# Moving the state matmuls of a fused attention and feed-forward kernel from around the transposes to between the gate/up pairs

## The chip, the core and the metric

The kernel runs on one core of a Trainium2 chip. A core has five engines that run their own instruction streams and meet at semaphores: TensorE (PE, matrix products into PSUM), VectorE (DVE), ScalarE (ACT), GpSimd (POOL) and SyncE (SP, which issues transfers). The metric is the device time of one execution in microseconds (us), the median of three runs: 507.38 us before the change (507.33 to 507.74).

## What is computed

The input `x` is 8 sequences of 1024 tokens with 256 channels, fp32. With `xn = layernorm(x)` the output is

```python
x + attn(xn) + ffn(xn)

# attn: linear attention with 16 heads of 16 channels
q = elu(xn @ Wq.T) + 1;  k = elu(xn @ Wk.T) + 1;  v = xn @ Wv.T
kv_state = einsum('bhnd,bhne->bhde', k, v);  k_state = k.sum(tokens)
attn_out = einsum('bhnd,bhde->bhne', q, kv_state) / max(einsum('bhnd,bhd->bhn', q, k_state), 1e-6)
local    = three-tap convolution of xn along the tokens, per channel
attn     = (attn_out + local) @ Wp.T + bp

# ffn: int weights times 1/127, hidden size 768
ffn = (silu(xn @ wg.T) * (xn @ wu.T)) @ wd.T
```

`kv_state` and `k_state` sum over all 1024 tokens of a sequence, so the attention output of a sequence can only be formed when all its keys and values have been seen.

## The kernel before

A sequence `b` is worked off in two halves `c = 0, 1` of 512 tokens, 16 halves in all, one after the other. Halves of sequences 2 to 6 stand in a hardware loop (`Fori`), the others are written out. fp32 precision comes from fp16 pairs: a tensor is held as a high and a low part (`xh`, `xl`), and a product is made as three fp16 products (two where a weight is exact in fp16).

In each half PE issues, in this order (function names as in the code):

- `project_kv(0)`, `query` for the same half of the sequence before (with `state`, as fp32), `project_kv(1)`, `project_q()`
- `accumulate(0)`: the state matmuls of the first two token tiles, `v_sb` with `k_sb` as 32-column weights in four column groups of the array, 16 instructions (32 in the trace) into PSUM bank 6
- `transpose_attn` twice: 8 transposes of `attn` into banks 5 and 7
- `accumulate(1)`: the state matmuls of the other two tiles
- `gate_up(0)` to `gate_up(5)`: each a gate/up pair of 8 matmuls of 512 columns into two PSUM banks. Even pairs use banks 2 and 3, odd ones 0 and 1. Between them stand `project_y` (after `gate_up(4)`, and after `gate_up(5)`)
- `down(0)`, `down(1)`: 48 matmuls of 256 columns

What the other engines do around these pairs sets when a pair may start. `gate_up(0)` waits for `v_ready`, `gate_up(1)` for `q_read` (DVE has read the banks of `project_q`), and every later `gate_up(j)` for `hid_ready` of pair `j-2`, because it overwrites the banks which that pair filled. After `project_q`, ACT runs `q_neg` (L526), `q_exp` (L529), loads the table for silu (L557), and then `silu(0)` (L536), which needs `gu_done` of pair 0. DVE runs `q_relu` (L858), `put_y` twice (L806), then `hidden(0)` (L896, makes `hid` from `act_g` and the up bank), `put_q` (L865), `hidden(1)` and so on.

`accumulate` waits for `k_ready`, `v_ready`, `acc_kept` and `attn_ready`. Its result is read by `put_state` on DVE (L873, L878), which stands behind `hidden_low(5)`; in the very last half, where nothing follows, it stands earlier, before `hidden(2)`. In that last half ("not ahead") `project_y` stands after `gate_up(2)` and after `gate_up(3)`, and the queries of the last sequence come after `gate_up(4)`.

Of the kernel before, what the change touches and what calls it, by code (L numbers as in the profile page):

```python
# [39 lines left out]
def build(nc, x, wqT, wkT, wvT, wpT, bp, conv_w, conv_b, wgT, wuT, wdT, out):  # L40
# [16 lines left out]
    def at(b, c, per_step, k):  # L57

        return b * (CB * per_step) + (c * per_step + k)

    with ExitStack() as ctx:
# [92 lines left out]
        def gate_bank(j):  # L154
            return 2 * ((j + 1) % 2)
# [873 lines left out]
        def _(pe):  # L1029
            def tiles_of(bank):  # L1030
                return ps[:, bank, :].rearrange("p (i t) -> p i t", i=TILES)
# [3 lines left out]
            def three(dst, stat, mov):  # L1035

                for n, (s, m) in enumerate(TERMS):
                    for k in range(KT):
                        ins = nc.tensor.matmul(dst, stat(s, k), mov(m, k), start=(n == 0 and k == 0),  # L1039
                                               stop=(n == len(TERMS) - 1 and k == KT - 1))  # L1040
                return ins
# [63 lines left out]
            def transpose_attn(b, c, p, banks):  # L1105

                pe.wait_ge(attn_ready, at(b, c, 2, p + 1))
                for i in range(2):
                    for k in range(KT):
                        ins = nc.tensor.transpose(ps[:, banks[p], k * PAIR + i * P:k * PAIR + (i + 1) * P],  # L1110
                                                  attn[:, 2 * p + i, k * P:(k + 1) * P], ident[:, :])
                ins.then_inc(yT_done, 1)

            def project_y(b, c, p, banks):
                pe.wait_ge(yl_ready, at(b, c, 2, p + 1))
                for i in range(2):
                    t = slice((2 * p + i) * P, (2 * p + i + 1) * P)
                    ins = three(ps[:, banks[p], i * D:(i + 1) * D], lambda s, k: (yh, yl)[s][:, k, t],
                                lambda m, k: p_w[m][:, k, :])
                ins.then_inc(wp_done, 1)  # L1120

            def step(b, c, attend, ahead):
# [27 lines left out]
                def accumulate(p):  # L1150

                    pe.wait_ge(k_ready, at(b, c, 2, p + 1))
                    pe.wait_ge(v_ready, at(b, c, 2, p + 1))
                    if p == 0 and past:

                        pe.wait_ge(acc_kept, at(b, c, 1, 0))
                    if p == 0 and attend:

                        pe.wait_ge(attn_ready, at(b - 1, c, 2, 2))
                    for i in (2 * p, 2 * p + 1):  # L1160
                        for k in range(KT):
                            for g in range(G):
                                rows = slice(g * GROUP, (g + 1) * GROUP)
                                ins = nc.tensor.matmul(ps[rows, STATE, k * VW:(k + 1) * VW],  # L1164
                                                       k_sb[:, i, k * P + g * GROUP:k * P + (g + 1) * GROUP],
                                                       v_sb[:, i, k * G + g, :], start=(i == 0 and k == 0),
                                                       stop=(i == TILES - 1), skip_group_check=True,
                                                       tile_position=(0, g * GROUP))
                    ins.then_inc(acc_done, 1)

                def project_q():

                    if past:
                        pe.wait_ge(v_ready, at(b, c, 2, 1))
                    else:
                        pe.wait_ge(first_xl, 1)
                        pe.wait_ge(q_hi, 1)
                        pe.wait_ge(q_lo, 1)
                    bank = 0 if past else FIRST_Q
                    for m in range(KT):  # L1180
                        ins = three(tiles_of(bank + m), lambda s, k: q_w[s][:, k, m * P:(m + 1) * P],
                                    lambda s, k: x2[s][:, c, :, k, :])
                    ins.then_inc(q_done, 1)

                def gate_up(j):

                    if j == 0:

                        pe.wait_ge(v_ready, at(b, c, 2, 2))
                    elif j == 1 and not past:  # L1190

                        pe.wait_ge(v_ready, 1)
                    elif j == 1:

                        pe.wait_ge(q_read, at(b, c, 1, 1))
                    else:
                        pe.wait_ge(hid_ready, at(b, c, J, j - 1))
                    for n, w in enumerate((g_w, u_w)):
                        dst = tiles_of(gate_bank(j) + n)
                        cols = slice(j * P, (j + 1) * P)  # L1200
                        for k in range(KT):
                            nc.tensor.matmul(dst, w[0][:, k, cols], xh[:, c, :, k, :], start=(k == 0), stop=False)  # L1202
                    with pe.If(is_wide["gate_up"]):
                        pe.wait_ge(gate_up_lo, 2)
                        for n, w in enumerate((g_w, u_w)):
                            for k in range(KT):
                                nc.tensor.matmul(tiles_of(gate_bank(j) + n), w[1][:, k, j * P:(j + 1) * P],
                                                 xh[:, c, :, k, :], start=False, stop=False)
                    for n, w in enumerate((g_w, u_w)):
                        for k in range(KT):  # L1210
                            ins = nc.tensor.matmul(tiles_of(gate_bank(j) + n), w[0][:, k, j * P:(j + 1) * P],  # L1211
                                                   xl[:, c, :, k, :], start=False, stop=(k == KT - 1))
                    ins.then_inc(gu_done, 1)
# [72 lines left out]
                    query(b - 1, c, 1, QKV)  # L1286
                project_kv(1)
                project_q()
                accumulate(0)
                if attend:  # L1290
                    transpose_attn(b - 1, c, 0, TURNED)
                    transpose_attn(b - 1, c, 1, TURNED)
                accumulate(1)
                gate_up(0)
                gate_up(1)
                if isinstance(b, int) and b == 1 and c == 0:

                    pe.wait_ge(p_hi, 1)
                    pe.wait_ge(p_lo, 1)
                if ahead:  # L1300
                    for j in range(2, J):
                        gate_up(j)
                        if attend and j == Y_PROJECT:

                            project_y(b - 1, c, 0, WP)
                    if attend:

                        project_y(b - 1, c, 1, WP)

                    pe.wait_ge(hid_ready, at(b, c, J, J - 1))  # L1310
                    down(0, DOWN)
                    if past and not attend:

                        pe.wait_ge(res_ready, at(b, c - 1, 2, 2))

                    down(1, DOWN)
                else:
                    first, second = 0, 1
                    gate_up(2)
                    project_y(b - 1, c, 0, WP)  # L1320
                    gate_up(3)
                    project_y(b - 1, c, 1, WP)
                    gate_up(4)

                    pe.wait_ge(out_ready, at(b - 1, c, 2, 2))
                    query(b, first, 0, LAST_QKV[0])
                    query(b, first, 1, LAST_QKV[0])
                    gate_up(5)

                    pe.wait_ge(hid_ready, at(b, c, J, J - 1))  # L1330
                    query(b, second, 0, LAST_QKV[1])
                    transpose_attn(b, first, 0, LAST_YT[0])

                    pe.wait_ge(hid_ready, at(b, c, J, J))
                    query(b, second, 1, LAST_QKV[1])
                    transpose_attn(b, first, 1, LAST_YT[0])
                    down(0, LAST_DOWN)

                    project_y(b, first, 0, LAST_WP[0])
                    project_y(b, first, 1, LAST_WP[0])  # L1340

                    transpose_attn(b, second, 0, LAST_YT[1])
                    transpose_attn(b, second, 1, LAST_YT[1])
                    down(1, LAST_DOWN)

                    project_y(b, second, 0, LAST_WP[1])
                    project_y(b, second, 1, LAST_WP[1])

            is_wide = {}
            run(pe, step)  # L1350


# [23 lines left out]
```

## Time and profile before

| | before |
|---|---|
| median of 3 runs | 507.38 us (507.33 to 507.74) |
| the profiled execution: its own time | 506.9 us |
| its span, first to last instruction | 505.3 us |
| mean granted TensorE clock | 0.999 of full speed |
| PE busy | 491.4 us, 97% |
| DVE busy | 430.5 us, 85% |
| ACT busy | 334.3 us, 66% |
| state matmuls (L1164) on the chain that ended last | 2.3% |

The profile is of one execution. "Busy" is the time in which an engine had an instruction in flight. A PE row of the timeline groups instructions that ran back to back; its duration includes the way of the last result through the array, so the step from one row's start to the next row's start is what a group costs PE in a stream, and the duration is longer than that. In brackets stands how long the engine was idle before a row and what ended the wait. PEld is the weight load of PE. Times in the timeline count from the start of the span.

### The profile page before, as it was taken

The numbers are of one execution on the slowest core, as the hardware profiler recorded it, in microseconds if no ns is written. First come the engines' busy times: TensorE is split into PE (matmuls) and PEld (weight loads), VectorE is DVE, ScalarE is ACT, GpSimd is POOL, SyncE is SP. The second block draws the span as 40 slices with busy tenths as digits, with TensorE's granted clock in tenths as the row PEclk, the third lists the DMA queues.
The fourth block names the chain that finished last, engine by engine and source line by source line (L and its number), as shares of the span: only waits on it lengthen the run. The fifth ranks groups of instructions, "written<-read, shape, count | busy, mean of one in ns | idle before, by whom it ended". The sixth has DMA issues, their size and how long they took to land.

```text
span 505.3 us, 11017 instructions
## 1 busy us (share of the span) xinstructions
PE 491.4 (97%) x3968; PEld 306.1 (61%) x3968; DVE 430.5 (85%) x833; ACT 334.3 (66%) x522; POOL 144.7 (29%) x152
## 2 busy tenths in 40 slices
PE   7888999999999999999999999999999999999997
PEld 6545364755747566474756657475565756657576
DVE  4889898889888898988889888889888889897786
ACT  2676866667485775757667485667758576674770
POOL 3563415140321405033140502314041141401050
PEclk9999999999999999999999999999999999999999
DMA  8573434333524423252352325233342442233012
GB/s 307 183 91 77 86 82 87 68 111 51 151 43 111 99 45 125 41 166 42 83 125 42 125 42 164 43 82 100 54 138 42 126 82 42 87 50 74 3 42 84
DMA packets 68653, 45.36 MB, mean 90 GB/s; under 512 B 33424, under 2 KB 68112, under 8 KB 68624
## 3 DMA queue, kind: packets, MB, share of 16 engines
q1 hardware_dynamic: 59360, 35.79, 25.2%
q0 software_dynamic: 8448, 8.39, 11.0%
q10 hardware_dynamic: 816, 0.79, 0.5%
q8 instruction: 19, 0.31, 0.3%
q14 instruction: 10, 0.08, 0.0%
HBM read 20.32 MB, written 8.39 MB: 57 GB/s over the span
## 4 chain that ended last, share of the span: by engine, by line
PE 88%; DVE 5%; ACT 3%; DMA 2%; issue 1%; ACTq 0%; DVEq 0%
PE ps L1202 16%; PE ps L1039 16%; PE ps L1211 15%; PE ps L1221 15%; PE ps L1145 15%; PE ps L1101 5%; PE ps L1110 3%; PE ps L1164 2%; DMA wv_raw<-in_L_attn_Wv_dram 2%; DVE maxima L665 1%; DVE hl L902 1%; DVE hid L896 1%; ACT hh L544 1%; DVE cb L764 0%; PE ps L1085 0%
## 5 line engine op out<-in xcount | busy, mean ns | idle before, releaser
L536 ACT ACTIVATE act_g<-ps,scales 128x512 f32<-128x512 f32 x96 | 65.9, 687 | 42.0 <-PE ps L1211 39.7
L896 DVE SCALAR_TENSOR_TENSOR hid<-act_g,scales,ps 128x512 f32<-128x512 f32 x96 | 71.4, 744 | 21.2 <-ACT act_g L536 20.7
L902 DVE TENSOR_TENSOR hl<-hid,hh 128x512 f16<-128x512 f32 x96 | 66.3, 691 | 1.8 <-ACT hh L544 0.4
L361 POOL TENSOR_TENSOR xT<-xh,xl 128x1024 f32<-128x1024 f16 x15 | 32.3, 2153 | 109.4 <-issue 109.4
L544 ACT ACTIVATE hh<-hid 128x512 f16<-128x512 f32 x96 | 59.7, 622 | 5.3 <-DVE hid L896 5.3
L1202 PE MATMUL ps<-xh,g_wh 128*128 128x512 f16 x192 | 57.6, 382 | 2.1 <-ACT u_wh L455 1.4
L1211 PE MATMUL ps<-xl,g_wh 128*128 128x512 f16 x192 | 57.1, 379 | 0.0
L1202 PE MATMUL ps<-xh,u_wh 128*128 128x512 f16 x192 | 57.1, 379 | 0.0
L1211 PE MATMUL ps<-xl,u_wh 128*128 128x512 f16 x192 | 57.1, 379 | 0.0
L1221 PE MATMUL ps<-d_wh,hh 128*128 128x256 f16 x384 | 52.4, 273 | 2.2 <-DVE hid L896 2.2
L499 ACT ACTIVATE k_neg<-ps,scales 128x512 f32<-128x512 f32 x30 | 20.6, 687 | 49.4 <-PE ps L1145 49.4
L1221 PE MATMUL ps<-d_wh,hl 128*128 128x256 f16 x384 | 52.7, 273 | 0.1
L326 POOL TENSOR_SCALAR xn<-x_in,neg_mean,rstd 128x256 f32<-128x256 f32 x62 | 51.5, 843 | 4.3 <-POOL rstd L333 4.2
L473 ACT ACTIVATE local<-xT,cb,cw 128x512 f32<-128x512 f32 x32 | 24.3, 807 | 42.3 <-POOL xT L361 39.3
L832 DVE SCALAR_TENSOR_TENSOR local<-xT,cw,local 128x512 f32<-128x512 f32 x60 | 45.2, 790 | 0.4 <-ACT local L473 0.4
L1221 PEld LDWEIGHTS ps<-d_wh,hh 128*128 128x128 f16 x384 | 37.3, 98 | 7.5 <-ACT hh L544 2.2
L1221 PEld LDWEIGHTS ps<-d_wh,hl 128*128 128x128 f16 x384 | 37.3, 98 | 5.1 <-DVE hl L902 0.7
L912 DVE SCALAR_TENSOR_TENSOR res<-ps,scales,xb 128x512 f32<-128x512 f32 x32 | 23.7, 746 | 17.3 <-PE ps L1221 17.3
L357 POOL TENSOR_TENSOR xT<-xh,xl 128x2 f32<-128x2 f16 x8 | 1.8, 224 | 122.2 <-DMA xl<-xn_l 85.8
L333 POOL TENSOR_TENSOR rstd<-var_eps,half 128x4 f32<-128x4 f32 x15 | 15.9, 1057 | 72.6 <-DVE var_eps L622 72.6
L1101 PEld LDWEIGHTS ps<-state,q_sb 128*128 128x128 f32 x256 | 32.1, 190 | 2.9 <-DVE hid L896 0.6
L1101 PE MATMUL ps<-state,q_sb 128*128 128x136 f32 x256 | 32.5, 279 | 0.3 <-DVE hid L896 0.3
(149 smaller groups left out, 965.5 us busy)
## 6 DMA issues: line engine op xcount, KB each, us to landing
xb<-bp_sb SPq DMA_DIRECT2D x16, 512.0 KB, 3.4
xb<-in_L_attn_x_dram POOLq DMA_DIRECT2D x16, 512.0 KB, 5.9
x_in<-in_L_attn_x_dram SPq DMA_DIRECT2D x15, 512.0 KB, 4.1
out_dram<-out_sb SPq DMA_DIRECT2D x14, 512.0 KB, 2.9
out_dram<-out_sb SPq DMA_DIRECT2D x4, 256.0 KB, 2.1
wg_int<-in_L_ffn_w_gate_dram SPq DMA_DIRECT2D x1, 768.0 KB, 7.1
wu_int<-in_L_ffn_w_up_dram SPq DMA_DIRECT2D x1, 768.0 KB, 8.6
wd_int<-in_L_ffn_w_down_dram SPq DMA_DIRECT2D x1, 768.0 KB, 11.1
```

Source lines behind the costliest of these rows:

```text
L326: return nc.gpsimd.tensor_scalar(xn[:, i, :], x_in[:, c, i, :], neg_mean[:, c, i:i + 1], rstd[:, c, i:i + 1], ALU.add, ALU.mult)
L536: nc.scalar.activation(act_g[:, j % 2, :], ps[:, gate_bank(j), :], ACT.Silu, scale=silu_in).then_inc(silu_ready, 1)
L544: nc.scalar.activation(hh[:, j, :], hid[:, j % 2, :], ACT.Copy).then_inc(hh_ready, 1)
L832: nc.vector.scalar_tensor_tensor(out=here, in0=xT[:, c, k, side:side + CHUNK], scalar=cw[:, k, side:side + 1], in1=here, op0=ALU.mult, op1 ...
L896: nc.vector.scalar_tensor_tensor(out=hid[:, j % 2, :], in0=act_g[:, j % 2, :], scalar=h_mul, in1=ps[:, gate_bank(j) + 1, :], op0=ALU.mult, ...
L902: nc.vector.tensor_tensor(hl[:, j, :], hid[:, j % 2, :], hh[:, j, :], ALU.subtract).then_inc(hl_ready, 1)
L1039: ins = nc.tensor.matmul(dst, stat(s, k), mov(m, k), start=(n == 0 and k == 0), stop=(n == len(TERMS) - 1 and k == KT - 1))
L1101: ins = nc.tensor.matmul(ps[:, banks[p] + i % 2, k * AW:(k + 1) * AW], q_sb[:, c, k, i * P:(i + 1) * P], state[:, k, :], start=True, stop= ...
L1145: ins = nc.tensor.matmul(ps[:, 2 * p + i, :], x2[s][:, c, 2 * p + i, k, :], kv_w[m][:, k, :], start=(n == 0 and k == 0), stop=(n == len(TE ...
L1202: nc.tensor.matmul(dst, w[0][:, k, cols], xh[:, c, :, k, :], start=(k == 0), stop=False)
L1211: ins = nc.tensor.matmul(tiles_of(gate_bank(j) + n), w[0][:, k, j * P:(j + 1) * P], xl[:, c, :, k, :], start=False, stop=(k == KT - 1))
L1221: ins = nc.tensor.matmul(ps[:, banks[p], i * D:(i + 1) * D], h[:, j, t], w[:, j, :], start=start and i == 0, stop=stop, skip_group_check=True)
```

## The change

The two calls of `accumulate` are moved within PE's program. Nothing else is changed, and no instruction is added or taken away on any engine; ACT, DVE and SP have the same order as before.

```diff
                 project_kv(1)
                 project_q()
-                accumulate(0)
                 if attend:
                     transpose_attn(b - 1, c, 0, TURNED)
                     transpose_attn(b - 1, c, 1, TURNED)
-                accumulate(1)
                 gate_up(0)
                 gate_up(1)
+                accumulate(0)
                 if isinstance(b, int) and b == 1 and c == 0:
 
                     pe.wait_ge(p_hi, 1)
...
                 if ahead:
                     for j in range(2, J):
                         gate_up(j)
+                        if j == 2:
+                            accumulate(1)
                         if attend and j == Y_PROJECT:
...
                 else:
                     first, second = 0, 1
                     gate_up(2)
+                    accumulate(1)
                     project_y(b - 1, c, 0, WP)
                     gate_up(3)
```

It acts on 15 of the 16 halves; the first half of the first sequence has an order of its own.

PE in a half of the loop, from the end of `project_q` to the start of `gate_up(0)`, before the change (L1164 is `accumulate`, L1110 `transpose_attn`, L1202 the first matmul of a gate/up pair; the register and ISA rows make the values that a wait compares with):

```order
L1039 MATMUL ps<-xl,q_wh 128x512 x2
L1159 ISA [waits acc_kept,v_ready,k_ready]
L1164 MATMUL ps<-v_sb,k_sb 32x33 [waits attn_ready]
L1164 MATMUL ps<-v_sb,k_sb 32x33 x15
L1107 REGISTER_ALU
L1110 MATMUL ps<-ident,attn 128x128 [waits attn_ready]
L1110 MATMUL ps<-ident,attn 128x128 x3
L1110 MATMUL ps<-ident,attn 128x128 [waits attn_ready]
L1110 MATMUL ps<-ident,attn 128x128 x3
L1152 REGISTER_ALU
L1164 MATMUL ps<-v_sb,k_sb 32x33 [waits v_ready,k_ready]
L1164 MATMUL ps<-v_sb,k_sb 32x33 x15
```

The same place after the change:

```order
L1039 MATMUL ps<-xl,q_wh 128x512 x2
L1107 ISA
L1110 MATMUL ps<-ident,attn 128x128 [waits attn_ready]
L1110 MATMUL ps<-ident,attn 128x128 x3
L1107 REGISTER_ALU
L1110 MATMUL ps<-ident,attn 128x128 [waits attn_ready]
L1110 MATMUL ps<-ident,attn 128x128 x3
L1189 REGISTER_ALU
L1202 MATMUL ps<-xh,g_wh 128x512 [waits v_ready]
```

Both groups of 16 state matmuls are gone from here, and `gate_up(0)` follows the transposes at once.

PE in the same half, between `gate_up(1)` and `gate_up(2)`, as a piece of the difference:

```order
 L1211 MATMUL ps<-xl,g_wh 128x512 x2
 L1211 MATMUL ps<-xl,u_wh 128x512 x2
+L1164 MATMUL ps<-v_sb,k_sb 32x33 [waits acc_kept,attn_ready,v_ready,k_ready]
+L1164 MATMUL ps<-v_sb,k_sb 32x33 x15
 L1197 REGISTER_ALU
 L1202 MATMUL ps<-xh,g_wh 128x512 [waits hid_ready]
```

The first group now stands directly ahead of the matmul that waits for `hid_ready`; the second group stands in the same way between `gate_up(2)` and `gate_up(3)`.

In the last half the second group comes ahead of `project_y` (PE, after the change, from the end of `gate_up(2)`):

```order
L1211 MATMUL ps<-xl,g_wh 128x512 x2
L1211 MATMUL ps<-xl,u_wh 128x512 x2
L1164 MATMUL ps<-v_sb,k_sb 32x33 [waits v_ready,k_ready]
L1164 MATMUL ps<-v_sb,k_sb 32x33 x15
L1039 MATMUL ps<-p_wh,yh 128x256 [waits yl_ready]
```

Before, the matmul of `project_y` followed `gate_up(2)` directly.

## Rows read from the trace of the kernel before

**Rows 1.** The page: busy time by engine, and the granted clock in 40 slices.
```profile
PE 491.4 (97%) x3968; PEld 306.1 (61%) x3968; DVE 430.5 (85%) x833; ACT 334.3 (66%) x522; POOL 144.7 (29%) x152
...
PEclk9999999999999999999999999999999999999999
```

**Rows 2.** Timeline of PE, half (3, 1): start, duration, engine, line, operation, count.
```profile
230.05 0.59 PE L1039 MATMUL ps<-xl,q_wh 128*128 128x512 f16 x2
230.57 0.46 PE L1164 MATMUL ps<-v_sb,k_sb 128*32 128x33 f32 x32
230.96 1.09 PE L1110 MATMUL ps<-ident,attn 128*128 128x128 f32 x8
231.99 0.46 PE L1164 MATMUL ps<-v_sb,k_sb 128*32 128x33 f32 x32
232.38 0.61 PE L1202 MATMUL ps<-xh,g_wh 128*128 128x512 f16 x2
...
234.12 0.59 PE L1202 MATMUL ps<-xh,g_wh 128*128 128x512 f16 x2
...
235.84 0.60 PE L1202 MATMUL ps<-xh,g_wh 128*128 128x512 f16 x2
...
237.64 0.60 PE L1202 MATMUL ps<-xh,g_wh 128*128 128x512 f16 x2
```

**Rows 3.** Timeline of ACT, the same half.
```profile
230.68 1.12 ACT L526 ACTIVATE q_neg<-ps,scales 128x1024 f32<-128x1024 f32 x1 [0.26 <-PE ps L1039]
...
232.91 1.28 ACT L557 ACT_TABLE_LOAD   x1
234.32 0.69 ACT L536 ACTIVATE act_g<-ps,scales 128x512 f32<-128x512 f32 x1
```

**Rows 4.** Timeline of DVE, the same half.
```profile
231.83 1.28 DVE L858 TENSOR_SCALAR q_relu<-ps,scales 128x1024 f32<-128x1024 f32 x1 [0.69 <-ACT q_neg L526]
...
235.04 0.75 DVE L896 SCALAR_TENSOR_TENSOR hid<-act_g,scales,ps 128x512 f32<-128x512 f32 x1 [0.60 <-ACT act_g L536]
...
236.84 0.74 DVE L896 SCALAR_TENSOR_TENSOR hid<-act_g,scales,ps 128x512 f32<-128x512 f32 x1
```

**Rows 5.** Timeline of PE, half (0, 0): `gate_up(0)` followed by state matmuls.
```profile
24.46 0.59 PE L1211 MATMUL ps<-xl,u_wh 128*128 128x512 f16 x2
24.98 0.77 PE L1164 MATMUL ps<-v_sb,k_sb 128*32 128x33 f32 x64
```

**Rows 6.** The chain that ended last, around the end: start, duration, what.
```profile
482.08 0.88 PE ps L1211 x4
...
495.62 0.87 PE ps L1110 x8
```

**Rows 7.** Timeline of PE, half (3, 0): `gate_up(1)` and `gate_up(2)`.
```profile
204.12 0.59 PE L1202 MATMUL ps<-xh,g_wh 128*128 128x512 f16 x2
...
206.02 0.60 PE L1202 MATMUL ps<-xh,g_wh 128*128 128x512 f16 x2
```

**Rows 8.** Timeline of ACT, half (3, 0): `silu(0)`.
```profile
204.40 0.69 ACT L536 ACTIVATE act_g<-ps,scales 128x512 f32<-128x512 f32 x1 [0.20 <-PE ps L1211]
```

**Rows 9.** Waits of PE, whole span: line, waited for; us in total, times, longest.
```profile
PE ps L1202 <- DVE hid L896: 0.2, 1, 0.2
```

**Rows 10.** Timeline of ACT, half (0, 1): table load and `silu(0)`.
```profile
55.02 1.28 ACT L557 ACT_TABLE_LOAD   x1
56.31 0.69 ACT L536 ACTIVATE act_g<-ps,scales 128x512 f32<-128x512 f32 x1
```

**Rows 11.** Timeline of PE, half (0, 1): pairs 1, 2 and 5, and `down(0)`.
```profile
56.05 0.60 PE L1202 MATMUL ps<-xh,g_wh 128*128 128x512 f16 x2 [0.45 <-DVE q_relu L858]
...
57.84 0.60 PE L1202 MATMUL ps<-xh,g_wh 128*128 128x512 f16 x2
...
63.22 0.60 PE L1202 MATMUL ps<-xh,g_wh 128*128 128x512 f16 x2
...
65.68 1.27 PE L1221 MATMUL ps<-d_wh,hh 128*128 128x256 f16 x10 [0.56 <-DVE hid L896]
```

## The prediction

> **What bounds the kernel now.** I read the page first. PE is busy for 97% of the span, at the full clock in all 40 slices [rows 1]. So a microsecond of PE work or of PE waiting that is added or taken away in the steady halves is a microsecond of time, unless something else is late at once. Next came PE's timeline in one steady half, (3, 1) [rows 2], read by the steps from start to start. The last two matmuls of project_q start at 230.05 and take 0.43 (2 of the 0.216 that a gate/up pair's 8 matmuls in 1.73 give each), so project_q leaves PE at Q = 230.48. The first state group starts at 230.57, the transposes at 230.96, the second state group at 231.99, gate_up(0) at 232.38, gate_up(1) at 234.12, gate_up(2) at 235.84, gate_up(3) at 237.64. From these:
>
> - entering state matmuls costs a gap: 0.09 after project_q (230.48 to 230.57). The gap after a gate/up pair is the same: in half (0, 0) the last matmuls start at 24.46, leave at 24.89, and the state matmuls start at 24.98 [rows 5].
> - one state group costs 0.39 (230.57 to 230.96; 231.99 to 232.38).
> - the 8 transposes take 1.03 here, but 0.87 at the end of the kernel where fp16 matmuls follow them [rows 6]. The other 0.16 is the entry into the second state group.
> - pairs 0 and 1 take 1.73 each, pair 2 takes 1.80: 0.07 of that is a wait.
>
> Third, ACT and DVE in the same half [rows 3, 4], for the chain that ends in hid_ready of pair 0, which gate_up(2) waits for. ACT starts q_neg at 230.68, 0.20 after Q. The table load starts at 232.91 and ends at 234.19. silu(0) starts at 234.32, its hidden(0) on DVE 0.72 later (235.04), and gate_up(2) 0.80 after that (235.84). silu(0) needs pair 0 too. That left PE at 234.12, and ACT sees it 0.20 later, at 234.32. So before the change the two conditions of silu(0), the table and pair 0, come within 0.13 of each other, and gate_up(2) starts just when PE has nothing else left: it is released by a chain that starts at Q and not by PE's own speed. This is the row that decides.
>
> **The change part by part.** No instruction is added. PE's work between Q and gate_up(2) shrinks by one state group, and that group stands between gate_up(2) and gate_up(3).
>
> *Entries and exits.* Before: 0.09 + 0.16 for two entries, 0.78 for two groups, 0.87 for the transposes, 1.90 in all (230.48 to 232.38). After: two entries of 0.09 from a gate/up pair, 0.78, 0.87, that is 1.83. If nothing waited, a half would gain 0.07. The state groups come later than before, so their own waits cost nothing. The transposes come 0.48 earlier, but the attn_ready they wait for was already there at 230.57, since the first state group waits for it too and started without a wait; I cost that at nothing as well. No row shows an entry from gate_up(1) in a steady half; its bounds are 0 and the 0.16 of the transposes, and I take 0.09, twice seen after 512-column matmuls.
>
> The row shows a gap at each entry and none at the exit: gate_up(0) after a state group keeps 1.73. The Trainium skill (TensorEngine Tiling (Array Packing), Key Properties) says that changing the tiling mode drains TensorE. By that rule each of four switches would cost, before as after, and the sum of switches would not move; by the rows the two exits are free and one entry gets cheaper by 0.07.
>
> *How early silu(0) can be.* The transposes now end at Q + 0.87, pair 0 at Q + 2.60 = 233.08. pair 1 waits for q_relu: it starts at 231.83 on DVE, behind q_neg and not behind PE, and lasts 1.28 [rows 4]; with 0.05 for the semaphore (in half (0, 1) gate_up(1) follows the same instruction in that way [rows 11]) pair 1 starts at 233.16, 0.08 late, which changes nothing below. silu(0) could have pair 0 at 233.28. But the table load still ends at 234.19, because q_neg, q_exp and the load hang on Q alone. How soon silu follows a load: in half (0, 1) the load ends at 56.30 and silu(0) starts at 56.31, with pair 0 long done (PE had been idle for 0.45 when it started pair 1 at 56.05) [rows 10, 11]. So silu(0) goes from 234.32 to 234.20: 0.12 earlier, and not the 1.0 by which PE is earlier.
>
> The rows have silu 0.13 and 0.01 after the end of the load. The Trainium skill (ScalarE: Activation LUTs, What ACT_TABLE_LOAD costs) gives about 1283 ns for the load and a drain of some 1380 ns behind it. With that drain silu(0) could not start before 235.57 and gate_up(2) not before 237.09; the load agrees (1.28), the drain does not show here, and I leave it out.
>
> *gate_up(2) and (3).* hidden(0) starts at 234.92 (DVE is free: it had been idle for 0.60 before 235.04), hid_ready reaches PE 0.80 later, gate_up(2) starts at 235.72. PE has finished pair 1 at 234.89 and the first state group at 235.37: **a new wait of 0.35**. Then 1.73 + 0.09 + 0.39: gate_up(3) starts at 237.93. Its own condition, hidden(1), stands on DVE behind put_q and moves with hidden(0): 236.84 - 0.12 + 0.80 = 237.52, early enough. Before it was 237.64. So a half is **0.29 longer**. Put otherwise: 0.39 + 0.09 of work moved behind the gate, minus 0.12 that the gate opens earlier, minus the 0.07 wait that it covers. Behind gate_up(3) PE shows no wait in these halves (in the whole span a gate/up pair waited for hid once for as long as 0.2 [rows 9], and the smaller ones are the 0.07 above), so PE stays the bound and the 0.29 is not given back. This holds in 8 halves: (1, 0), (1, 1), (2, 1) to (6, 1), (7, 0). 8 x 0.29 = 2.32.
>
> *The five loop halves (2, 0) to (6, 0).* Here gate_up(1) starts at 204.12, silu(0) at 204.40, 0.28 later where (3, 1) has 0.20, and gate_up(2) at 206.02, 1.62 after silu(0) where (3, 1) has 1.52 [rows 7, 8]. That makes 1.90 from gate_up(1) to gate_up(2), 0.17 of it wait. The table load ends 0.07 after gate_up(1) starts in (3, 1); by the same step it ends at 204.19 here. After: silu(0) at 204.20 to 204.28 (whether the 0.08 stays), and gate_up(2) 1.52 to 1.62 later, at 205.72 to 205.90 and gate_up(3), 2.21 later, at 207.93 to 208.11, where before it came 1.80 after 206.02 by the step of rows 2, at 207.82. That is 0.11 to 0.29; I take 0.22, near the end at which the delays stay. 5 x 0.22 = 1.10.
>
> *Half (0, 1)* has no transposes and no queries. gate_up(1) starts at 56.05, released by q_relu after a wait of 0.45 [rows 11]; that stays, with the wait now 0.78 and more longer, so the groups taken from ahead of it give nothing. Behind it: pair 1 to 57.78, entry and group to 58.26, where gate_up(2) stood at 57.84; then 1.73 + 0.48 to gate_up(3) at 60.47, gate_up(4) at 62.20, gate_up(5) at 63.93, where it stood at 63.22. Of the 0.84 added behind gate_up(1), waits of before cover 0.13; +0.71. down(0) at 65.68 is itself released by a hidden part that hangs on pair 4, so it moves along. Bounds 0.4 and 0.84.
>
> *The last half (7, 1).* As in the others up to gate_up(2) (-0.12, with the wait), then 0.48 ahead of project_y, where before was no wait: +0.36. The chain runs on PE up to the end of gate_up(4) [rows 6], so it counts in full.
>
> The sum: 2.32 + 1.10 + 0.71 + 0.36 = 4.49. The profiled execution took 506.9 (span 505.3): 511.4. The median of the runs is 0.48 above that execution, so against it: **511.9**.
>
> Ends of the sum. Low: entries free and the loop halves at the lower end, 8 x 0.20 + 5 x 0.02 + 0.55 + 0.27 = 2.5, or 509.9. High: entries 0.16 each and the loop halves at the upper end, 8 x 0.36 + 5 x 0.36 + 0.84 + 0.50 = 6.1, or 513.5.
>
> **The rivals.**
>
> *A: the waits go (faster).* If silu(0) followed pair 0 rather than the table, hid_ready would come some 0.9 earlier, the state groups would fill PE's small waits, and each half would gain 0.07 of entries and 0.07 of waits, the loop halves another 0.17: 14 x 0.14 + 5 x 0.17 = 2.8, or 504.6. For it: gate_up(2) and (3) do wait a little before, and there the change puts work. Against it: rows 10 show silu starting 0.01 after a load with its pair done; nothing in ACT's order moves. It decides for faster when hid_ready of pair 0 comes before Q + 4.89. 6%.
>
> *B: the wait is there but is given back.* If ACT or DVE, not PE, set the pace from gate_up(3) to the next half, PE's 0.29 would vanish in their slack: 507.4, at most 508.4 with half (0, 1) and the last. For it: DVE is 85% busy [rows 1]. Against it: were another engine the pace there, PE would wait behind gate_up(3) in every half, and rows 9 leave no room for that. 8%.
>
> *C: the same mechanism, but costlier.* The state groups cut the stream of weight loads twice more among pairs whose loads run ahead, and the loop halves keep all their delays: the high end, 513.5 or somewhat more. 14%.
>
> **How the numbers follow.** The forecast, 0.02 to 0.36 per half, has 72%, its time 511.9, its own range 509.9 to 513.5. With C both slower; B lies within 0.2% or just above; A is faster. Against 507.38 the 0.2% that a measurement can tell is 1.0 us. Slower: 0.72 + 0.14 + a quarter of B = 0.88; same 0.06; faster 0.06. The range for 8 in 10 takes both ends with a little of B and C: 509.6 to 513.6.
>
> **What would show it.** In the steady halves: gate_up(2) starts at Q + 5.24 (before 5.36) with PE idle for some 0.35 ahead of it, released by hid; gate_up(3) at Q + 7.45 (before 7.16); silu(0) starts 0.01 after the table load with PE long done; the transposes step 0.87. In half (0, 1) gate_up(5) 0.7 later. The table load's place against Q must not have moved. Wrong it would be if silu(0) started before the load's end, if gate_up(2) started without a wait, or if gate_up(4) or (5) stood where they stood before against Q.

## The result and the profile after

The changed kernel takes 512.25 us (median of 6 runs, 511.55 to 512.75), the kernel before 507.68 on the same chips (6 runs, 507.33 to 507.90): a ratio of 1.0095, 95% interval 1.0085 to 1.0105. The forecast was 511.9, in a range of 509.6 to 513.6. The profiled execution took 512.06 with a span of 510.4, so the span grew by 5.1.

The page after: busy time by engine and the granted clock (as [rows 1]).

```profile
PE 491.9 (96%) x3968; PEld 307.7 (60%) x3968; DVE 432.3 (85%) x833; ACT 334.9 (66%) x522; POOL 145.1 (28%) x152
...
PEclk9999999999999999999999999999999999999999
```

PE's busy time grew by 0.5 only, at the same clock. The rest of the 5.1, 4.6, is idle time of PE. Its waits name it (line, waited for; us in total, times, longest), to be held against [rows 9]:

```profile
PE ps L1202 <- DVE hid L896: 4.4, 15, 0.3
...
PE ps L1202 <- DVE q_relu L858: 1.6, 1, 1.6
```

Before, a gate/up pair waited for `hid` once for 0.2; now 15 times, 4.4 in total. The wait for `q_relu` is the one of half (0, 1), 0.45 before ([rows 11]) and longer now because state work is gone from ahead of it. The timeline of PE in half (3, 1), against [rows 2]:

```profile
232.55 0.59 PE L1039 MATMUL ps<-xl,q_wh 128*128 128x512 f16 x2
232.98 1.04 PE L1110 MATMUL ps<-ident,attn 128*128 128x128 f32 x8
233.86 0.59 PE L1202 MATMUL ps<-xh,g_wh 128*128 128x512 f16 x2
...
235.68 0.61 PE L1202 MATMUL ps<-xh,g_wh 128*128 128x512 f16 x2
...
237.51 0.46 PE L1164 MATMUL ps<-v_sb,k_sb 128*32 128x33 f32 x32
238.23 0.61 PE L1202 MATMUL ps<-xh,g_wh 128*128 128x512 f16 x2 [0.26 <-DVE hid L896]
...
240.06 0.46 PE L1164 MATMUL ps<-v_sb,k_sb 128*32 128x33 f32 x32
240.45 0.60 PE L1202 MATMUL ps<-xh,g_wh 128*128 128x512 f16 x2
```

ACT in the same half (before: [rows 3]):

```profile
233.19 1.12 ACT L526 ACTIVATE q_neg<-ps,scales 128x1024 f32<-128x1024 f32 x1 [0.26 <-PE ps L1039]
...
235.41 1.28 ACT L557 ACT_TABLE_LOAD   x1
236.71 0.69 ACT L536 ACTIVATE act_g<-ps,scales 128x512 f32<-128x512 f32 x1
```

DVE (before: [rows 4]):

```profile
234.34 1.28 DVE L858 TENSOR_SCALAR q_relu<-ps,scales 128x1024 f32<-128x1024 f32 x1 [0.68 <-ACT q_neg L526]
...
237.43 0.75 DVE L896 SCALAR_TENSOR_TENSOR hid<-act_g,scales,ps 128x512 f32<-128x512 f32 x1 [0.49 <-ACT act_g L536]
...
239.22 0.74 DVE L896 SCALAR_TENSOR_TENSOR hid<-act_g,scales,ps 128x512 f32<-128x512 f32 x1
```

`project_q` ends at Q = 232.98. The table load ends at 236.69, and `silu(0)` starts at 236.71, though pair 0 left PE at 235.59. `gate_up(2)` starts at Q + 5.25, after PE had finished the first state group at 237.90. In the list of instructions PE shows 0.26 of idle there, counted from the last result; counted from the end of the group's 0.39 it is 0.33. Then come pair 2, the entry, the second group, and `gate_up(3)` at Q + 7.47.

The starts of the gate/up pairs after the end of `project_q`, worked out in the same way from the timeline of PE in all halves:

| half | kernel | pair 0 | pair 1 | pair 2 | pair 3 | pair 5 |
|---|---|---|---|---|---|---|
| (3, 1), as (1, 1), (2, 1), (4, 1) to (7, 0) in their kind | before | 1.90 | 3.64 | 5.36 | 7.16 | 11.93 |
| | after | 0.88 | 2.70 | 5.25 | 7.47 | 12.25 |
| (3, 0), as (2, 0) to (6, 0) | before | 1.90 | 3.63 | 5.53 | 7.32 | 12.09 |
| | after | 0.87 | 2.69 | 5.33 | 7.55 | 12.32 |
| (0, 1) | before | 1.11 | 3.46 | 5.25 | 7.04 | 10.63 |
| | after | 0.00 | 3.46 | 5.69 | 7.91 | 11.38 |
| (7, 1) | before | 1.89 | 3.63 | 5.36 | 8.40 | 15.02 |
| | after | 0.87 | 2.69 | 5.24 | 8.78 | 15.40 |

The sum over the halves at pair 5: 7 x 0.31, (1, 0) 0.37, 5 x 0.23, (0, 1) 0.75, (7, 1) 0.38, in all 4.8. The other 0.3 of the 5.1 comes before the first changed instruction: `project_q` of half (0, 1) ends at 52.59 before and at 52.89 after. In the traces of the kernels below, whose PE program is the same up to there, that point lies anywhere from 52.58 to 54.07, and in two traces of one and the same kernel (both groups ahead of `gate_up(2)`) at 54.07 and 53.22. It is a spread of the start, and no effect of the change.

### The profile page after: what moved, and what is told of

Its sections match the earlier page's. It is cut to its first block, busy times and chain, and to the rows that moved or that the text cites. A ratio compares the mean times of both kernels' runs of the same rounds, so it can differ in the third digit from the quotient of the medians.

```text
span 510.4 us, 11027 instructions
## 1 busy us (share of the span) xinstructions
PE 491.9 (96%) x3968; PEld 307.7 (60%) x3968; DVE 432.3 (85%) x833; ACT 334.9 (66%) x522; POOL 145.1 (28%) x152
## 4 chain that ended last, share of the span: by engine, by line
PE 74%; ACT 9%; DVE 7%; issue 7%; DMA 2%; ACTq 0%; DVEq 0%
PE ps L1039 15%; PE ps L1145 15%; PE ps L1221 15%; PE ps L1202 11%; PE ps L1211 10%; PE ps L1101 5%; ACT q_neg L526 3%; DVE hid L896 3%; ACT act_g L536 2%; DMA wv_raw<-in_L_attn_Wv_dram 2%; PE ps L1164 1%; ACT L557 1%; DVE hl L902 1%; DVE maxima L665 1%; ACT hh L544 0%
## 5 line engine op out<-in xcount | busy, mean ns | idle before, releaser
L902 DVE TENSOR_TENSOR hl<-hid,hh 128x512 f16<-128x512 f32 x96 | 68.2, 711 | 1.7 <-ACT hh L544 0.4
L1202 PE MATMUL ps<-xh,g_wh 128*128 128x512 f16 x192 | 57.6, 382 | 7.4 <-DVE hid L896 4.4
L1202 PE MATMUL ps<-xh,u_wh 128*128 128x512 f16 x192 | 57.1, 379 | 0.0
```

The source lines that it names most:

```text
L902: nc.vector.tensor_tensor(hl[:, j, :], hid[:, j % 2, :], hh[:, j, :], ALU.subtract).then_inc(hl_ready, 1)
```

## The experiments

Two theories stood against each other. **G**, the gate: `gate_up(2)` may start only when `hidden(0)` is done, and that chain starts at the end of `project_q` and not behind PE's own work; state matmuls moved behind the gate no longer fill the time up to it. ("The gate" is this point in PE's program; it has nothing to do with the gate weights of a gate/up pair.) **S**, the switch: every entry of the 32-column state matmuls into the stream of gate/up pairs costs. On PE, half (0, 1) has the order of before in all experiments, so they speak of the 14 halves with attention. Each median of before was measured beside the run that it is held against.

### Only the second group moved

```diff
                     transpose_attn(b - 1, c, 1, TURNED)
-                accumulate(1)
+                if not attend:
+                    accumulate(1)
                 gate_up(0)
...
                         gate_up(j)
+                        if attend and j == 2:
+                            accumulate(1)
```

and the same behind `gate_up(2)` of the last half.

> Only the second state group is moved, behind gate_up(2); the first stays between project_q and the transposes. Half (0, 1), which has no transposes, keeps its old order. Theory G (gate_up(2) is gated by a chain that starts when project_q ends: q_neg, q_exp, table load, silu(0), hidden(0); only what stands behind that gate costs): PE's work ahead of the gate is 4.8 us after the end of project_q against a gate at 5.25, so gate_up(2) still waits (some 0.4) and gate_up(3) starts at 7.45 as in the full change. 8 x 0.31 + 5 x 0.23 + 0.38 = 4.0 over the kernel before. Rival S (what costs is each entry of 32-column matmuls into the stream of gate/up pairs): one of two such entries, so half, 2.0 over before.

Measured: 511.51 against 507.26, ratio 1.0085 (1.0072 to 1.0099), +4.25. PE in half (3, 1) of this kernel, where Q is 232.16:

```profile
232.26 0.46 PE L1164 MATMUL ps<-v_sb,k_sb 128*32 128x33 f32 x32
232.65 1.09 PE L1110 MATMUL ps<-ident,attn 128*128 128x128 f32 x8
233.58 0.59 PE L1202 MATMUL ps<-xh,g_wh 128*128 128x512 f16 x2
...
235.30 0.59 PE L1202 MATMUL ps<-xh,g_wh 128*128 128x512 f16 x2
...
237.41 0.61 PE L1202 MATMUL ps<-xh,g_wh 128*128 128x512 f16 x2 [0.22 <-DVE hid L896]
...
239.24 0.46 PE L1164 MATMUL ps<-v_sb,k_sb 128*32 128x33 f32 x32
239.63 0.60 PE L1202 MATMUL ps<-xh,g_wh 128*128 128x512 f16 x2
```

`gate_up(2)` at Q + 5.25 and `gate_up(3)` at Q + 7.47: the same two numbers as with the full change, with one group in its old place. Moving the second group alone has the whole cost of these halves (the offsets at pair 5 add up to 4.1 here and in the next run alike); S wanted half of it.

### The change in the halves with attention only

```diff
+                if not attend:
+                    accumulate(0)
+                    accumulate(1)
                 if attend:
                     transpose_attn(b - 1, c, 0, TURNED)
                     transpose_attn(b - 1, c, 1, TURNED)
                 gate_up(0)
                 gate_up(1)
-                accumulate(0)
+                if attend:
+                    accumulate(0)
...
-                        if j == 2:
+                        if attend and j == 2:
                             accumulate(1)
```

(against the changed kernel)

> The full change in the 14 halves with attention; half (0, 1) keeps its old order. G and S alike: 4.0 over the kernel before, that is 0.7 less than the full change, if half (0, 1) costs the 0.75 that the traces show; a second reading, that half (0, 1) is given back later, has it at 4.7.

Measured: 511.76 against 507.26, ratio 1.0086 (1.0072 to 1.0099), +4.5. The interval, 3.7 to 5.0 us, holds both readings, so the time doesn't tell them apart. The trace speaks for the first: from the end of `project_q` in half (0, 1) to the same point in the last half it takes 420.69 where the full change takes 421.48, and in half (0, 1) pair 5 starts at Q + 10.62 again.

### Both groups together, ahead of gate_up(2)

```diff
-                accumulate(0)
+                if not attend:
+                    accumulate(0)
+                    accumulate(1)
                 if attend:
                     transpose_attn(b - 1, c, 0, TURNED)
                     transpose_attn(b - 1, c, 1, TURNED)
-                accumulate(1)
                 gate_up(0)
                 gate_up(1)
+                if attend:
+                    accumulate(0)
+                    accumulate(1)
```

> Both state groups together between gate_up(1) and gate_up(2) (14 halves; half (0, 1) as before). G: nothing stands behind the gate; PE reaches gate_up(2) at 5.22 after project_q's end (0.87 + 1.73 + 0.10 + 1.73 + 0.09 + 0.70), the gate opens at 5.25 (5.33 in the loop's first halves); gate_up(3) follows at 7.04 (7.13), by hidden(1), where before has 7.16 (7.32). 8 x 0.12 + 5 x 0.19 + 0.11 = 2.0 faster than before. S: an entry among the pairs in each half, 2.0 slower than before.

Measured: 505.21 against 507.26, ratio 0.9957 (0.9943 to 0.9970), 2.05 faster than before. The same kernel once more:

> The kernel with both state groups between gate_up(1) and gate_up(2) once more, on the same chip as the run with put_q moved in the attention halves: 2.0 faster than before.

505.46 against 507.56, ratio 0.9960 (0.9947 to 0.9974), 2.1 faster. PE in half (3, 1) of the first of these runs, Q = 231.25:

```profile
231.25 1.04 PE L1110 MATMUL ps<-ident,attn 128*128 128x128 f32 x8
232.13 0.59 PE L1202 MATMUL ps<-xh,g_wh 128*128 128x512 f16 x2
...
233.95 0.60 PE L1202 MATMUL ps<-xh,g_wh 128*128 128x512 f16 x2
...
235.78 0.76 PE L1164 MATMUL ps<-v_sb,k_sb 128*32 128x33 f32 x64
236.50 0.60 PE L1202 MATMUL ps<-xh,g_wh 128*128 128x512 f16 x2
...
238.29 0.61 PE L1202 MATMUL ps<-xh,g_wh 128*128 128x512 f16 x2
```

There is an entry among the pairs in each half here, and the kernel is faster than before. All state work now stands ahead of the gate. `gate_up(2)` starts at Q + 5.25, as it does in the changed kernel, but `gate_up(3)` at Q + 7.04 instead of 7.47. The offsets at pair 5 are 0.11 to 0.20 below those of before and add up to 2.0. S falls.

### Both groups together, ahead of gate_up(0)

```diff
                     transpose_attn(b - 1, c, 1, TURNED)
+                if attend:
+                    accumulate(0)
+                    accumulate(1)
                 gate_up(0)
                 gate_up(1)
-                if attend:
-                    accumulate(0)
-                    accumulate(1)
```

(against the kernel of the last section)

> Both state groups together between the transposes and gate_up(0) (14 halves; half (0, 1) as before). G: the place ahead of the gate does not matter, only that the groups are joined: gate_up(0) at 0.87 + 0.16 + 0.70 = 1.73 after project_q's end (before 1.90), gate_up(2) at 5.25, as in the run with both between gate_up(1) and gate_up(2), 2.0 faster than before. S: no entry among the pairs, at most 14 x 0.09 = 1.3 faster than before and 3 faster than that run.

Measured: 505.73 against 507.26, ratio 0.9968 (0.9956 to 0.9980), 1.5 faster than before, and within the intervals the same as with the groups between `gate_up(1)` and `gate_up(2)`. Its PE in half (3, 1), Q = 229.75:

```profile
229.75 1.04 PE L1110 MATMUL ps<-ident,attn 128*128 128x128 f32 x8
230.72 0.77 PE L1164 MATMUL ps<-v_sb,k_sb 128*32 128x33 f32 x64
231.43 0.60 PE L1202 MATMUL ps<-xh,g_wh 128*128 128x512 f16 x2
...
234.99 0.60 PE L1202 MATMUL ps<-xh,g_wh 128*128 128x512 f16 x2
...
236.79 0.61 PE L1202 MATMUL ps<-xh,g_wh 128*128 128x512 f16 x2
```

`gate_up(2)` at Q + 5.24, `gate_up(3)` at Q + 7.04. Ahead of the gate the place makes no difference; behind it, it costs. This run also shows where the gain of the joined groups comes from and what limits it: `gate_up(0)` starts at Q + 1.68 instead of 1.90, 0.22 earlier, and `gate_up(2)` only 0.12 earlier, because the gate opens no sooner.

### The gate taken away: relu in the place of silu

```diff
-                    nc.scalar.activation(act_g[:, j % 2, :], ps[:, gate_bank(j), :], ACT.Silu,
+                    nc.scalar.activation(act_g[:, j % 2, :], ps[:, gate_bank(j), :], ACT.Relu,
...
-                nc.scalar.preload_act_table(ACT.Silu)
...
-                    nc.scalar.preload_act_table(ACT.Exp)
```

Both kernels of this section compute another function than the one asked for; they serve to time the order alone. First with the order of before, as a base:

> The order of before, but relu stands in the place of silu (the output is another), and the two table loads of each half are gone. The base for the next run. G: silu(0) needs pair 0, which it had only 0.13 after the table, so the gate stays at 5.36 after project_q's end and the time moves little: 0 to 1.5 less than before. S says nothing of it.

Measured: 507.32 against 507.54, ratio 1.0005 (0.9996 to 1.0014), no change. In half (3, 1) the pairs start at the offsets of before within 0.01 (5.36 and 7.15 after Q), because in that order `silu(0)` waits for pair 0 anyway.

Then with the order of the change in the 14 halves with attention:

> The order of the change (14 halves; half (0, 1) as before), with relu in the place of silu and no table loads (the output is another). G: without the load the chain is 1.28 shorter, the gate opens at about 4.7 after project_q's end, before PE gets there at 4.91; gate_up(2) does not wait, gate_up(3) starts at 7.13. So the change costs nothing against the run with relu in the old order: 0 to 1.5 faster than it. S: the entries among the pairs are still there, 4.0 slower than that run.

Measured: 506.74, against 507.32 for the base measured beside it, 0.6 faster than it; the ratio to the kernel before is 0.9990 (0.9981 to 0.9999). ACT in half (3, 1), Q = 230.41 (line numbers of PE and DVE in this kernel are 2 lower):

```profile
231.76 1.06 ACT L529 ACTIVATE q_exp<-q_neg 128x1024 f32<-128x1024 f32 x1
233.22 0.69 ACT L536 ACTIVATE act_g<-ps,scales 128x512 f32<-128x512 f32 x1 [0.40 <-PE ps L1209]
```

PE in the same half, the first matmuls of pairs 1, 2 and 3:

```profile
233.10 0.61 PE L1200 MATMUL ps<-xh,g_wh 128*128 128x512 f16 x2
...
235.33 0.61 PE L1200 MATMUL ps<-xh,g_wh 128*128 128x512 f16 x2
...
237.55 0.60 PE L1200 MATMUL ps<-xh,g_wh 128*128 128x512 f16 x2
```

PE's waits for `hid` ahead of a gate/up pair, whole span:

```profile
PE ps L1200 <- DVE hid L894: 0.2, 1, 0.2
```

The activation now starts when pair 0 is there (released by PE, 2.81 after Q), `gate_up(2)` starts at Q + 4.92 as soon as PE has finished the first group, and `gate_up(3)` at Q + 7.14, 0.01 ahead of the base and 0.02 ahead of before. The 4.4 of waits are back to 0.2. The order of PE is that of the change in all these halves, with both entries among the gate/up pairs, and it costs nothing. So the cost of the change is the wait at the gate and not the order as such.

### The second gate: put_q behind hidden(1)

With both groups ahead of `gate_up(2)`, `gate_up(3)` still starts 1.79 after it instead of 1.73. On DVE:

```diff
                         hidden(j)
-                        if j == 0:
+                        if j == 1:
                             put_q()
```

> Both state groups between gate_up(1) and gate_up(2), and on DVE put_q behind hidden(1) instead of behind hidden(0) (in all halves but the last). G: gate_up(3) was still held for some 0.06 by hidden(1), which stood behind the 1.2 of put_q; with that gone it follows gate_up(2) at once: 13 x 0.06 = 0.8 faster than with both groups there alone, some 2.8 faster than before. If hidden_low(0), now later, holds hidden(2) up, the 0.8 is lost or worse.

Measured: 505.59 against 507.54, ratio 0.9970 (0.9958 to 0.9982), 1.95 faster than before and not 2.8. The wait goes: pairs 2 and 3 start at 5.24 and 6.98 after Q in half (3, 1). But pair 5 gains 0.03 only (11.79 where it was 11.82), since `gate_up(4)` is now held by `hidden(2)` (it starts 1.76 after pair 3). And half (0, 1) loses. DVE there:

```profile
59.53 0.75 DVE L896 SCALAR_TENSOR_TENSOR hid<-act_g,scales,ps 128x512 f32<-128x512 f32 x1 [0.93 <-ACT act_g L536]
60.19 1.22 DVE L865 TENSOR_TENSOR q_sb<-q_exp,q_relu 128x1024 f32<-128x1024 f32 x1
61.33 0.68 DVE L902 TENSOR_TENSOR hl<-hid,hh 128x512 f16<-128x512 f32 x1
62.12 0.75 DVE L896 SCALAR_TENSOR_TENSOR hid<-act_g,scales,ps 128x512 f32<-128x512 f32 x1
```

PE there:

```profile
62.92 0.60 PE L1202 MATMUL ps<-xh,g_wh 128*128 128x512 f16 x2 [0.64 <-DVE hid L896]
```

`hidden(2)` stands behind `put_q` and `hidden_low(0)`, and `gate_up(4)` starts at Q + 9.51 instead of 8.78: 0.6 lost at pair 5. The expectation named the late `hidden_low(0)` as the risk, but its price lay in half (0, 1) and not in the steady halves.

The same with `put_q` left behind `hidden(0)` in half (0, 1):

```diff
-                        if j == 1:
+                        if j == (1 if attend else 0):
                             put_q()
```

> As the run with both groups between gate_up(1) and gate_up(2) and put_q behind hidden(1), but put_q is moved only in the 13 halves with attention that are not the last; in half (0, 1) it stays behind hidden(0). There the later put_q had pushed hidden_low(1) and with it gate_up(4) 0.7 back in the trace. G: that 0.6 to 0.7 comes back; the steady halves keep their 0.03 and 0.06 each. 0.5 faster than both groups alone, 2.4 to 2.6 faster than before. If the moved put_q costs elsewhere in the steady halves, no faster than both groups alone.

Measured: 504.96 against 507.56, ratio 0.9951 (0.9937 to 0.9965), 2.6 faster than before and 0.5 faster than both groups alone (505.46 measured beside it, 504.85 to 506.00). The size is the one expected, but the intervals of the two overlap, so the time alone doesn't show it. The traces put the gain at 0.4: pair 5 of the loop's first halves starts at 11.85 instead of 11.90, of the seven others like (3, 1) at 11.79 instead of 11.81, and from the end of `project_q` in half (1, 0) to that in the last half it takes 386.27 instead of 386.66. Half (0, 1) is back at 10.63, as with both groups alone. It is the fastest of the kernels tried.

## Why the prediction was right

Point by point, in its own terms:

- *PE is the bound, nothing is given back.* Right. The shift that stands at `gate_up(3)` still stands at `gate_up(5)` (0.31 and 0.32 in half (3, 1)), and the span grew by the sum of the shifts. Rival B would have had pair 5 at its old offset.
- *silu(0) moves by 0.12 and no more.* Right: 3.73 after Q, before 3.84, with pair 0 done 1.0 earlier. It starts 0.02 after the load. The drain behind a table load that the Trainium skill gives (ScalarE: Activation LUTs, What ACT_TABLE_LOAD costs) would, as an estimate from its figure, have put it 1.4 later. It doesn't show here: in all nine traces with silu, an activation that waits for nothing else starts 0.01 to 0.02 after a load.
- *gate_up(2) at Q + 5.24, gate_up(3) at Q + 7.45.* Measured 5.25 and 7.47. *Pair 1 held 0.08 by q_relu, without effect*: `q_relu` ends at 235.62, pair 1 starts at 235.68, 1.82 after pair 0, and the relu run shows that `gate_up(2)` is then reached at Q + 4.92 (4.89 in the prediction).
- *Entries.* Predicted 0.09 after a gate/up pair, measured 0.10: 237.41 to 237.51 and 239.96 to 240.06 in half (3, 1). The exits to a gate/up pair are free, as predicted. The exit into the transposes is not: it costs 0.06, and the entry behind them 0.10, where the prediction had 0 and 0.16 (last section); the sum is the same, so the forecast did not suffer. The Trainium skill has TensorE drain at a change of tiling mode (TensorEngine Tiling (Array Packing), Key Properties). The gaps of 0.10 and 0.06 agree with that, the exits to a gate/up pair show none, and the relu run shows that such passages did not decide.
- *The loop's first halves, 0.22.* Measured 0.23, with some luck: 0.22 was a choice between 0.11 and 0.29, made without a mechanism. Of the two delays of 0.08 to 0.1 there, that of `silu(0)` vanished behind the table load, and that between `silu(0)` and `gate_up(2)` stayed: 1.61 in the changed kernel, 1.62 before. Their cause stays open.
- *Half (0, 1), 0.71*: 0.75. *Last half, 0.36*: 0.38. *Half (1, 0), 0.29*: 0.37. The prediction counted it with (3, 1) without a row of its own. The delay of 0.08 behind `silu(0)` stands there before and after (`gate_up(2)` at 5.45 and 5.33); before, it cost nothing, because `gate_up(3)` followed after 1.73 without a wait, where (3, 1) had 1.80.
- The sum was 4.49, the traces have 4.8, the medians 4.6. The missing 0.3 are 0.01 to 0.02 in each of the twelve halves like (3, 1) and (3, 0), 0.08 in (1, 0), 0.04 in (0, 1) and 0.02 in the last half.
- Slips in the working that didn't move the forecast: for half (0, 1) the text speaks of 0.84 added and 0.13 covered, where its own steps have two groups with their entries, 0.96, and 0.25 of waits covered (the difference, 0.71, is the same). The low end of the sum uses 0.55 for that half and not the 0.4 named as its bound, the high end uses 0.50 for the last half where one dearer entry gives 0.43, and its terms add up to 6.0 and not 6.1.

Rival A, the waits go and the kernel gets faster, named as its condition that `hid_ready` comes before Q + 4.89. The relu run meets it (`hidden(0)` starts at 3.87 after Q, which with the 0.80 to `gate_up(2)` is 4.67), and there the change is indeed no loss. So its condition failed in this kernel because of the table load. Its price was wrong as well: even without the load a half like (3, 1) gains 0.02 and not 0.14, since the 0.09 by which `q_relu` now holds pair 1 takes most of it. Rival C, costlier entries, is refuted by the entries themselves, 0.10 each; the run with both groups between `gate_up(1)` and `gate_up(2)` has one among the pairs in each half and gains.

## What to carry to other kernels

On a saturated engine, find the first instruction that is released by a chain which does not run over the engine's own recent work, and keep all independent filler ahead of that gate. Filler moved behind it costs its full time, less what the move saves ahead of it (here 0.49 of work moved behind it in a half with attention, and these halves became 0.23 to 0.38 longer). To place the gate, follow the chain back to the last point at which it hangs on the engine (here the end of `project_q`, then ACT's table load), and compare its offset (5.25) with the work the engine has up to there (5.36 before, 4.92 after the change). The two groups of 32-column matmuls, each of which changes the form of the array, were better joined than spread in this kernel: joined ahead of the gate they gained 0.3 to 0.4%.

## What was not expected of the hardware

- Joined state groups cost less than twice one group: 64 matmuls take 0.71 (230.72 to 231.43, joined ahead of `gate_up(0)`) with one entry, two groups of 32 take 0.39 each with two entries.
- An entry after the fp32 transposes costs 0.10 when no state group stands ahead of them (229.75 + 0.87 to 230.72), where [rows 2, 6] give 0.16 for it between two groups. The prediction had taken all of that 0.16 as an entry. In the run with only the second group moved, transposes that follow a state group and precede a gate/up pair take 0.93 (232.65 to 233.58), so 0.06 of the 0.16 belongs to the passage from state matmuls into the transposes, and the entry is 0.10 as elsewhere.
- Taking the table loads of 1.28 off ACT (31 instructions fewer in the trace, 10986 for 11017) did not change the time of the kernel with the old order (507.32 against 507.54), since there PE and not ACT holds the activation.
